# A graph layer on one core: messages and scan terms kept in PSUM, half of the features at a time

## The reference

```python
h = maximum(layernorm(x), 0)
xl = einsum('ni,nio->no', h, hetero_w[node_type]) + hetero_b[node_type]
ete = lrelu(edge_type_emb[edge_type]);  eae = lrelu(edge_attr @ edge_attr_w)
alpha = lrelu(concat([xl[dst], xl[src], ete, eae]) @ att_w)
alpha = exp(alpha - segment_max(alpha, dst)[dst])
alpha = alpha / (segment_sum(alpha, dst)[dst] + 1e-16)
msg = concat([xl[src], eae]) @ lin_w * alpha
out = x + segment_sum(msg, dst)
```

## Time and profile before

| | us |
|---|---|
| median of 3 runs | 4131.49 (4130.97 to 4132.56) |
| the profiled execution, its own time | 4129.91 |
| its span, first to last instruction | 4128.0 |
| POOL busy | 3089.6 (75%) |
| PE busy | 2477.6 (60%) |
| DVE busy | 2456.1 (59%) |
| ACT busy | 877.7 (21%) |
| mean granted clock of PE | 0.817 |

### The profile page before, as it was taken

The page is one execution under the profiler, slowest core; times in us unless marked ns, Lnnn a source line. Parts: engine busy times, 40 slices in busy tenths (PEclk is TensorE's granted clock), DMA queues, the critical chain, the costliest instruction groups (busy, mean ns, idle before and its releaser), DMA issues.

```text
span 4128.0 us, 50812 instructions
## 1 busy us (share of the span) xinstructions
PE 2477.6 (60%) x14238; PEld 1775.3 (43%) x14238; DVE 2456.1 (59%) x6517; ACT 877.7 (21%) x2080; POOL 3089.6 (75%) x2993
## 2 busy tenths in 40 slices
PE   4476666566566665665665665666656656656510
PEld 3354444444444444444444444444444444444410
DVE  5776565565565665665655656656655656656535
ACT  2131221221221221221222222222222222122100
POOL 0777777777777777777777777777777777777757
PEclk9798788888788888887888888888888888888855
DMA  6432222222222222222222222222222222222122
GB/s 179 110 82 63 58 70 60 58 72 58 58 73 58 60 70 58 67 63 58 71 59 58 72 58 58 73 58 63 67 58 68 62 58 72 58 58 72 27 59 72
DMA packets 194060, 275.76 MB, mean 67 GB/s; under 512 B 78284, under 2 KB 149310, under 8 KB 193152
## 3 DMA queue, kind: packets, MB, share of 16 engines
q1 hardware_dynamic: 72864, 150.69, 12.1%
q0 software_dynamic: 96768, 59.05, 10.5%
q10 hardware_dynamic: 24288, 64.79, 4.3%
HBM read 202.07 MB, written 72.22 MB: 66 GB/s over the span
## 4 chain that ended last, share of the span: by engine, by line
POOL 67%; issue 22%; PE 5%; DVE 3%; DMA 2%; POOLq 1%; SPq 0%; DVEq 0%; ACT 0%; ACTq 0%
POOL gath L491 64%; PE ps_misc L694 2%; POOL hib L531 1%; DMA gath<-table_dram,meta 1%; PE ps_pick L707 1%; DVE node_buf L1145 1%; PE ps_misc L661 1%; POOL hi_f L531 0%; POOL dst_f L531 0%; POOL node_buf L531 0%; PE ps_msg L739 0%; POOLq L488 0%; DVE dscore L1063 0%; PE ps_attr L716 0%; DMA rlast_i<-row_last_in 0%
## 5 line engine op out<-in xcount | busy, mean ns | idle before, releaser
L491 POOL DMA_INDIRECT gath<-table_dram,meta x2875 | 2979.3, 1036 | 969.7 <-issue 869.1
L694 PE MATMUL ps_misc<-parts,dst_f 128*128 128x462 bf16 x5250 | 1124.2, 371 | 239.8 <-DVE h L1050 232.3
L694 PEld LDWEIGHTS ps_misc<-parts,dst_f 128*128 128x128 bf16 x5250 | 514.4, 100 | 787.1 <-DVE h L1050 258.4
L1113 DVE TENSOR_TENSOR node_buf<-gath,ps_msg 128x495 f32<-128x495 f32 x125 | 83.8, 671 | 1132.7 <-DMA gath<-table_dram,meta 1132.7
L750 PE MATMUL ps_msg<-hi_f 128*128 128x98 bf16 x625 | 70.1, 271 | 1105.6 <-DVE node_buf L1115 1105.6
L1063 DVE TENSOR_REDUCE dscore<-ps_pick 128x4 f32<-128x512 f32 x875 | 537.4, 629 | 195.9 <-PE ps_pick L707 195.9
L707 PE MATMUL ps_pick<-s_dst,onehot 122*128 122x128 f32 x3000 | 592.6, 374 | 18.9 <-DVE dscore L1063 17.8
L591 ACT ACTIVATE wts<-args 128x50 f32<-128x50 f32 x125 | 30.7, 246 | 2585.8 <-DVE args L1132 2585.8
L707 PEld LDWEIGHTS ps_pick<-s_dst,onehot 122*128 122x128 f32 x3000 | 560.4, 281 | 42.9 <-DVE dscore L1063 21.7
L750 PEld LDWEIGHTS ps_msg<-hi_f 128*128 128x128 bf16 x625 | 47.0, 127 | 1157.5 <-issue 1156.7
L707 PE MATMUL ps_pick<-s_dst,dst_f 122*128 122x128 f32 x3000 | 382.2, 276 | 21.3 <-DVE dscore L1063 21.3
(11 more groups left out here) (231 smaller groups left out, 1892.6 us busy)
## 6 DMA issues: line engine op xcount, KB each, us to landing
hib<-digit_dram SPq DMA_DIRECT2D x125, 612.5 KB
rows_dram<-rows ACTq DMA_DIRECT2D x125, 437.5 KB, 5.5
gath<-table_dram,meta POOLq DMA_INDIRECT x2875
attr<-edge_attr_t_in SPq DMA_DIRECT2D x125, 200.0 KB
hib<-digit_dram SPq DMA_DIRECT2D x250, 50.0 KB
rows_dram<-gath ACTq DMA_DIRECT2D x1, 8575.0 KB, 47.0
dst_f<-sel_code_dram SPq DMA_DIRECT2D x125, 64.0 KB, 5.3
hib<-digit_dram SPq DMA_DIRECT2D x250, 25.0 KB
```

The source lines that it names most:

```text
L491: nc.gpsimd.indirect_dma_start(gath[u][:, t, :], None, table_dram, bass.IndirectOffsetOnAxis(ap=meta_sb[u][:, t:t + 1], axis=0)).then_inc( ...
L694: last = nc.tensor.matmul(ps_sel[:, j % 2, 0:VW * GN], sel_onehot[:, g, j * P:(j + 1) * P], parts[:, k, g, :], start=(g == 0 and k == 0), ...
```

## The change

The messages are added in place, into ps_msg. terms is no longer in SBUF: it takes bank 1 of ps_misc, where 17 features x 26 columns fit, so products and scan are done in two halves, features 0 to 15 and then 16 to 32 (the last is the weight itself). Both selects now use bank 0, so the second waits until the product of the first is read. The signs, whose place in ps_msg must not be overwritten while messages stand there, go to bank 1 of ps_pick; PE makes them before the second select and not after the messages' addition, DVE takes them up after the exponents of the same chunk, and group 1 of the next chunk's scores waits for that. msg_used tells when a half has read the messages. The core of the diff:

```diff
-        msg = in_node_buf(2 * TG * P, [T, VW])
-        terms = in_node_buf(2 * TG * P + T * VW, [VW, T + 1])
-        ps_sel = ps_misc
-        ps_signs = ps_msg[:, 1, 2 * G * VW:2 * G * VW + NPP]
+        ps_sel = ps_misc[:, 0, 0:VW * GN]
+        terms = ps_misc[:, 1, 0:HALF * (T + 1)].rearrange("p (f t) -> p f t", t=T + 1)
+        halves = ((0, F_IN // 2), (F_IN // 2, VW))
+        ps_signs = ps_pick[:, 1, 0:NPP]
+        msg_parts = [(ps_msg[:, b, 0:n * VW].rearrange("p (t f) -> p t f", f=VW), slice(3 * G * b, 3 * G * b + n))
+                     for b, n in enumerate((3 * G, 2 * G))]
...
-                pe.wait_ge(sel_read, count(selected(i, u) + (j - 1 if j > 1 else 0)))
+                pe.wait_ge(sel_read, count(selected(i, u) + j))
...
+                if g == 1:
+                    pe.wait_ge(signs_summed, count(c))
...
-                pe.wait_ge(msg_added, count(c))
-                pe.wait_ge(signs_summed, count(c + 1))
+                pe.wait_ge(msg_used, count(2 * c))
...
-                if not final:
-                    select(*after, 1)
-
                 pe.wait_ge(signs_ready, c + 1)
-                pe.wait_ge(msg_added, count(c + 1))
+                pe.wait_ge(picked, count(c * PICKS + SIGNS_AFTER + 1))
                 for t in range(BPC):
                     last = nc.tensor.matmul(ps_signs, sign_hi[:, t, :], sign_lo[:, t, :], start=(t == 0),
                                             stop=(t == BPC - 1))
                 last.then_inc(signs_mm, 1)
+                if not final:
+                    select(*after, 1)
...
-                v.tensor_tensor(msg[:, 0:3 * G, :], gath[u][:, 0:3 * G, 0:VW],
-                                ps_msg[:, 0, 0:3 * G * VW].rearrange("p (t f) -> p t f", f=VW), ALU.add)
-                v.tensor_tensor(msg[:, 3 * G:T, :], gath[u][:, 3 * G:T, 0:VW],
-                                ps_msg[:, 1, 0:2 * G * VW].rearrange("p (t f) -> p t f", f=VW),
-                                ALU.add).then_inc(msg_added, 1)
+                for part_of_it, tiles in msg_parts:
+                    last = v.tensor_tensor(part_of_it, gath[u][:, tiles, 0:VW], part_of_it, ALU.add)
+                last.then_inc(msg_added, 1)
...
-                k = step(v.tensor_tensor(alpha[:], msg[:, :, F_IN], dscore[:], ALU.add))
+                for part_of_it, tiles in msg_parts:
+                    last = v.tensor_tensor(alpha[:, tiles], part_of_it[:, :, F_IN], dscore[:, tiles], ALU.add)
+                k = step(last)
...
+                sum_signs(c)
                 dve.wait_ge(sums_ready, count(c))
-                v.tensor_copy(terms[:, :, 0:1], sums[:, :, T:T + 1])
...
-                v.tensor_copy(terms[:, F_IN, 1:T + 1], wts[:, 0, :])
-                k = step(v.tensor_tensor(terms[:, 0:F_IN, 1:T + 1].rearrange("p f t -> p t f"), msg[:, :, 0:F_IN],
-                                         wts[:, 0, :].unsqueeze(2).broadcast_to([P, T, F_IN]), ALU.mult))
...
-                v.tensor_tensor_scan(sums[:].rearrange("p f t -> p (f t)"), keep[:].rearrange("p f t -> p (f t)"),
-                                     terms.rearrange("p f t -> p (f t)"), 0.0, ALU.mult,
-                                     ALU.add).then_inc(sums_ready, 1)
+                for n, (f0, f1) in enumerate(halves):
+                    fn = min(f1, F_IN)
+                    v.tensor_copy(terms[:, 0:f1 - f0, 0:1], sums[:, f0:f1, T:T + 1])
+                    if n == 0:
+                        dve.wait_ge(exp_done, c + 1)
+                    else:
+                        v.tensor_copy(terms[:, F_IN - f0, 1:T + 1], wts[:, 0, :])
+                    for part_of_it, tiles in msg_parts:
+                        last = v.tensor_tensor(
+                            terms[:, 0:fn - f0, 1 + tiles.start:1 + tiles.stop].rearrange("p f t -> p t f"),
+                            part_of_it[:, :, f0:fn], wts[:, 0, tiles].unsqueeze(2).broadcast_to(
+                                [P, tiles.stop - tiles.start, fn - f0]), ALU.mult)
+                    last.then_inc(msg_used, 1)
+                    if n == 0:
+                        dve.wait_ge(keep_ready, c + 1)
+                        dve.wait_ge(rows_sums, count(c))
+                    dve.wait_ge(msg_used, count(2 * c + n + 1))
+                    last = v.tensor_tensor_scan(sums[:, f0:f1, :].rearrange("p f t -> p (f t)"),
+                                                keep[:, f0:f1, :].rearrange("p f t -> p (f t)"),
+                                                terms[:, 0:f1 - f0, :].rearrange("p f t -> p (f t)"), 0.0, ALU.mult, ALU.add)
+                    if n == 0:
+                        need(step(last), at)
+                last.then_inc(sums_ready, 1)
```

More of the change, by code:

```diff
@@ L34 @@
 PICKS = -(-T // PICK_T)
+SIGNS_AFTER = PICKS - 2
 PART_AT = (0, 12, 24, T)
@@ L49 @@
 RW = F_IN + 3
+HALF = VW - F_IN // 2
 META = 2 * T + 1
@@ L300, in gnn_kernel @@
         msg_added = sem("msg_added")
+        msg_used = sem("msg_used")
         onehot_ready = sem("onehot_ready")
@@ L690, in select @@
                 pe.wait_ge(sel_onehot_ready if j else sel_first_ready, i * U + u + 1)
-                pe.wait_ge(sel_read, count(selected(i, u) + (j - 1 if j > 1 else 0)))
+                pe.wait_ge(sel_read, count(selected(i, u) + j))
                 for g in range(NG):
                     for k in range(3):
-                        last = nc.tensor.matmul(ps_sel[:, j % 2, 0:VW * GN], sel_onehot[:, g, j * P:(j + 1) * P],
+                        last = nc.tensor.matmul(ps_sel, sel_onehot[:, g, j * P:(j + 1) * P],
                                                 parts[:, k, g, :], start=(g == 0 and k == 0),
@@ L795, in _ @@
             dve.sem_inc(tab_sb, 2)
-            start_at_one(dve, maskT_sb, eae_ready, signs_summed, picked, msg_added, sums_ready, sel_read)
+            start_at_one(dve, maskT_sb, eae_ready, signs_summed, picked, msg_added, msg_used, sums_ready, sel_read)
             steps = [0]
@@ L854, in _ @@
             v.memset(no_rows[:, :, VW + 1:RW], -1.0).then_inc(node_rows_ready, 1)
-            v.memset(ps_signs, 0.0)
             done(v.memset(mrun[:], 0.0))
@@ L1049, in take_product @@
                 dve.wait_ge(sel_mm, count(selected(i, u) + j + 1))
-                v.tensor_tensor(sel_prod, ps_sel[:, j % 2, 0:VW * GN].rearrange("p (f n) -> p f n", n=GN),
+                v.tensor_tensor(sel_prod, ps_sel.rearrange("p (f n) -> p f n", n=GN),
                                 sel_mask[:, j:j + 1, :].broadcast_to([P, VW, GN]), ALU.mult).then_inc(sel_read, 1)
@@ L1066, in sum_signs @@
             def sum_signs(c):
-                dve.wait_ge(signs_mm, count(c))
+                dve.wait_ge(signs_mm, count(c + 1))
                 dve.wait_ge(signs_summed, count(c))
@@ L1089, in chunk @@
                 picks(c, 1)
-                sum_signs(c)
                 dve.wait_ge(eae_scaled, c + 1)
@@ L1135, in chunk @@
                     place(1, *after, at)
+                sum_signs(c)
                 dve.wait_ge(sums_ready, count(c))
-                v.tensor_copy(terms[:, :, 0:1], sums[:, :, T:T + 1])
                 if not final:
                     place(2, *after, at)
-                if not final:
                     place(3, *after, at)
-                dve.wait_ge(exp_done, c + 1)
-                v.tensor_copy(terms[:, F_IN, 1:T + 1], wts[:, 0, :])
-                k = step(v.tensor_tensor(terms[:, 0:F_IN, 1:T + 1].rearrange("p f t -> p t f"), msg[:, :, 0:F_IN],
-                                         wts[:, 0, :].unsqueeze(2).broadcast_to([P, T, F_IN]), ALU.mult))
@@ L1147, in chunk @@
-                dve.wait_ge(keep_ready, c + 1)
-                dve.wait_ge(rows_sums, count(c))
-                need(k, at)
-                v.tensor_tensor_scan(sums[:].rearrange("p f t -> p (f t)"), keep[:].rearrange("p f t -> p (f t)"),
-                                     terms.rearrange("p f t -> p (f t)"), 0.0, ALU.mult,
-                                     ALU.add).then_inc(sums_ready, 1)
+                for n, (f0, f1) in enumerate(halves):
[20 more added lines that the diff above has]
+                        need(step(last), at)
@@ L1173, in _ @@
                 chunk(ITERS - 1, u, 0, u == U - 1)
-            sum_signs(CHUNKS)
-            dve.wait_ge(signs_summed, count(CHUNKS + 1))
+            dve.wait_ge(signs_summed, count(CHUNKS))
             done(v.tensor_copy(sign_parts[:, 0, :], sign_sums[:]))
```

## The result

The changed kernel takes 3985.74 us (median of 4 runs, 3985.16 to 3988.01) against 4132.02 us (4130.97 to 4133.73, 4 runs) for the kernel before: a ratio of 0.9647, with a 95% interval from 0.963 to 0.9663. The profiled execution took 3985.32 us, its span 3983.5. Forecast were 3968 us, in a range from 3950 to 4006.

A forecast was written before the change was run, and what follows sets the result against it. GpSimd's gathers were taken to bound the loop, number times duration. From 4129.9 us: -169.7 (two stalls) +5 (third stall) +1.3 (end) = 3966.5; timed median 1.6 above, so 3968, range 3950 to 4006.

The forecast's parts named there:

- The two stalls: Gathers stretched beside the messages' multiplication and the scan, which read two SBUF tensors: both stalls go, -169.7 us.
- the scan holds the port all the same: Rival: the scan still stretches gathers with a PSUM source; only 68.9 us go, 4069 us, chance 0.05.
- it doesn't do what it says: Rival: product and scan both still stretch gathers; about 4138 us, no change or a little slower, chance 0.04.
- The third stall: Gathers stretched beside the two large comparisons: stays, 0.68 us a chunk for 0.643, +5 us, bounds -9 and +47.
- the tail: Behind the last gather, VectorE's added work lies bare once: +1.3 us; the tail's 98 gathers are untouched.
- VectorE's own work: VectorE's added work between L1113 and L1050: +1.3 us a chunk, covered by its wait for gathers, which shrinks to 4.6.
- my two estimates: Four products in place of one on VectorE: 1.1 or 2.2 us a chunk, against 1.68.
- TensorE's clock: A shorter TensorE burst after L1113 may leave the clock low; the first select block takes 7.04 us, not 4.28: +2.8.
- the rival of 4344 us: TensorE stays at clock 0.5, 32.4 us a chunk, and sets the time; with other TensorE/VectorE loops 0.04, 0.02 above today.
- Signs of the forecast: Expected in the changed kernel's profile: gathers' mean about 979 ns, chunks 29.3 to 29.4 us, POOL idle on issue alone.
- The one long gather a chunk that I had named: Sign: a single long gather remains in each chunk, beside the comparisons at L1082 (old L1078).

The follow-up runs named there:

- terms_sbuf: Changed kernel with terms put back into SBUF, messages left in PSUM: 4903.42 us, ratio 1.0557 to a kernel before of 4646.47.
- fill4: Changed kernel with one more VectorE reduction of about 4.1 us per chunk, ahead of the wait for gathered rows: 4943.31 us, ratio 1.0627.
- both_sbuf: Changed kernel with messages and terms both back in SBUF, only the order by halves kept: 4902.54 us, ratio 1.055; second time 4994.72, ratio 1.0267.
- msg_sbuf: Changed kernel with messages put back into SBUF, terms left in PSUM: 4857.39 us, ratio 1.0433.
- before_code_psum: Kernel before with its one-hot comparisons reading the row numbers from a PSUM column: 4694.59 us, ratio 1.0091.
- code_psum_4: Changed kernel with one-hot comparisons reading row_code from a PSUM column, fourth occasion: 4858.38 us, ratio 0.9979 to a kernel before of 4866.96.

## Why the prediction was right, and which term was mis-sized

*The two stalls.* Forecast -169.7 us; the count gives -169.7: no gather that touches a product or a half scan of the changed kernel is above 0.961 us. The rivals "the scan holds the port all the same" and "it doesn't do what it says" are refuted. The reason was right: that a source in PSUM frees the gathers is shown for the scans by terms_sbuf against the changed kernel, and for the products by the 63 gathers of fill4. It was not the only thing at work: the prediction gave no share to the order by halves, which takes away some 60 of the 169.7 us even with both tensors in SBUF. Whether PSUM without the halves would bring all of it wasn't run.

*The third stall*, the step that was mis-sized: "+5 us; bounds -9 and +47". It cost 101.4 - 80.4 = +21.0 us. I took 0.68 us a chunk as the mean over all places; the changed kernel sits at the dear ones, 0.81. The bounds held it. This is 16 of the 18.8 us between 3966.5 and the profiled 3985.32. The others: the first gather starts 1.5 us later, the first 54 gathers are 1.1 us longer and those beside the selects' one-hots 0.8, and the tail took 0.8 us less than I had added.

*VectorE's own work.* From L1116 to L1054 it is 2015.95 - 2009.19 = 6.76 us, from L1113 to L1050 it was 6.49: +0.27, not +1.3. The four products took 181.8 us in all, 1.45 us a chunk, between my two estimates (1.1 and 2.2) and under the 210.2 of the one before; the half scans cost 262.0 against 243.2. It did not matter, since the wait at L1116 is 6.5 us still; I had 4.6.

*TensorE's clock.* Foreseen in kind: 123 of the 250 blocks of select matmuls last over 5 us, 24 did before, and the block in the timeline above took 7.01 us. The clock fell to 0.783, not to 0.5, and POOL's idle time didn't grow; TensorE's 2592.4 us are 20.7 a chunk of 29.5, and the rival of 4344 us is refuted here. Its condition was put too high: TensorE would set the time from 29.4 us a chunk on, POOL's own; 30.7 is only where the gain would be used up.

*Signs of the forecast.* Gathers' mean 985 ns for 979, a chunk of 29.53 us for 29.3 to 29.4 (23 x 1.248 + 0.81 = 29.5), no wait of POOL in the loop: as written, but for the one term. The one long gather a chunk that I had named is two in 79 of the 125 chunks.

## What to carry to other kernels

Where GpSimd's gathers set the time, look at what VectorE reads while a gather starts: give one of two SBUF sources a place in PSUM, or cut the instruction so that gathers rarely begin inside it. A stall term must be priced at the place where the gathers will fall after the change. The mean over all places is a poor guess, since the places bunch (64 of 125 chunks within 0.3 us here); keep both ends in the range. Before a ratio is used, look at what the kernel before took beside that very run, and at whether the bounding engine is still the same in the trace.

## What the runs showed that I had not expected

*A destination in PSUM made the transposing product faster.* The products of 240 elements, in both_sbuf, msg_sbuf and the changed kernel by form:

```profile
L1153 DVE TENSOR_TENSOR node_buf<-node_buf,wts 128x240 f32<-128x240 f32 x250 | 153.1, 612 | 0.1
```

```profile
L1153 DVE TENSOR_TENSOR ps_misc<-node_buf,wts 128x240 f32<-128x240 f32 x250 | 101.1, 404 | 0.0
```

It takes 612 ns into SBUF, 606 from PSUM into SBUF (terms_sbuf), 404 from SBUF into PSUM and 405 from PSUM into PSUM. The source makes next to no difference, the destination a third. The write goes with a stride of 26 elements (104 bytes) here.

*The kernel before at 4650 and at 4880 us.* Four of the five occasions, on four chips, had it so in all of their runs; the fifth, on another chip, had 4151 us. Whether it belongs to the chip or to the occasion can't be told from this. In the traces of the four TensorE and VectorE show waits that the first traces don't have, here VectorE's score reduction in before_code_psum, against 195.9 us of idle time in the kernel before:

```profile
L1065 DVE TENSOR_REDUCE dscore<-ps_pick 128x4 f32<-128x512 f32 x875 | 534.5, 629 | 1277.9 <-remote 1041.1 <-PE ps_pick L708 194.3 <-issue 42.3
```

SyncE's five loads of hib, in the trace of the kernel before and in that of code_psum_4:

```profile
2057.18 2.13 SPq L369 DMA_DIRECT2D hib<-digit_dram  x5
```

```profile
2322.76 8.50 SPq L375 DMA_DIRECT2D hib<-digit_dram  x5
```

In these rows issuing them takes 8.5 us in place of 2.1. POOL then waits 955.8 us for the score reduction (the code_psum_4 row above) and is the bound no more. Kernels that keep the new order took up to 6% longer than the kernel before there, or the same (ratios 0.995 to 1.063). What delays the engines' streams stays open.
